# Second graph layer of a fused GNN + mixture-of-experts kernel: every engine's steps written out in an order of its own

## The reference

```
h = (_layernorm(x) * rsqrt(deg_out)); agg = segment_sum(h[src], dst)
h = (agg * rsqrt(deg_in)) @ W + b
x = x + gelu(_layernorm(h) * gamma + beta)                 # third sub-layer
xn = _layernorm(x); idx1 = argmax(xn @ w_gating)           # fourth: the expert of each row
pos1 = rank of the row among the rows with the same expert # its slot
out = x + gate1 * (gelu(_layernorm(xn) * gamma @ w1[idx1]) @ w2[idx1])
```

## Time and profile before

| | us |
|---|---|
| median of the runs | 965.11 |
| the profiled execution, its own time | 967.83 |
| its span, first to last instruction | 966.1 |
| PE busy over the span | 854.0 (88%) |
| DVE busy | 576.1 (60%) |
| ACT busy | 368.2 (38%) |
| POOL busy | 216.9 (22%) |
| granted PE clock, mean over the span | 0.942 of 2.4 GHz |

### The profile page before, as it was taken

The page is one execution under the profiler, slowest core; times in us unless marked ns, Lnnn a source line. Parts: engine busy times, 40 slices in busy tenths (PEclk is TensorE's granted clock), DMA queues, the critical chain, the costliest instruction groups (busy, mean ns, idle before and its releaser), DMA issues.

```text
span 966.1 us, 15966 instructions
## 1 busy us (share of the span) xinstructions
PE 854.0 (88%) x5064; PEld 572.6 (59%) x5064; DVE 576.1 (60%) x1871; ACT 368.2 (38%) x674; POOL 216.9 (22%) x425
## 2 busy tenths in 40 slices
PE   5989988989999999999997299999749999862996
PEld 2455554447777777777776277777414457452664
DVE  7488888338888787777773245555435325793121
ACT  1233434446665666666653133443200022231332
POOL 5000000000022012210222322222156213554443
PEclk9989999999999999999998599999959999965999
DMA  8239999972221024111008545653133440524550
GB/s 248 95 96 248 271 241 259 262 193 79 57 72 48 28 85 161 49 29 48 23 23 277 187 128 150 174 156 98 66 87 86 128 142 8 187 65 111 150 179 27
DMA packets 86979, 121.27 MB, mean 126 GB/s; under 512 B 40269, under 2 KB 49645, under 8 KB 86637
## 3 DMA queue, kind: packets, MB, share of 16 engines
q1 hardware_dynamic: 73293, 102.08, 38.0%
q0 software_dynamic: 13600, 18.11, 6.6%
HBM read 65.78 MB, written 57.08 MB: 127 GB/s over the span
## 4 chain that ended last, share of the span: by engine, by line
PE 72%; DVE 10%; issue 5%; DMA 4%; ACT 3%; POOL 3%; SPq 2%; DVEq 0%; POOLq 0%; ACTq 0%
PE ps L680 17%; PE ps L573 10%; PE ps L602 10%; PE ps L744 9%; PE ps L584 7%; PE ps L474 6%; PE ps L687 4%; PE ps L431 2%; PE ps L769 2%; DVE R_B L1419 2%; SPq L281 1%; DVE R_A L1517 1%; ACT R_B L893 1%; ACT R_A L888 1%; PE ps L639 1%
## 5 line engine op out<-in xcount | busy, mean ns | idle before, releaser
L680 PE MATMUL ps<-R_B,R_A 128*128 x612 | 186.0, 446 | 3.0 <-ACT R_A L1099 1.1
L680 PEld LDWEIGHTS ps<-R_B,R_A 128*128 128x128 f32 x612 | 111.9, 194 | 34.7 <-issue 24.6
L959 ACT ACTIVATE R_A<-R_A,neg_max 125x1250 f32<-125x1250 f32 x80 | 106.6, 1332 | 58.0 <-DVE neg_max L1517 58.0
L1517 DVE CUSTOM_DVE_ANT_0 R_A<-ps,R_B,neg_max 125x417 f32<-125x417 f32 (+1 forms) x160 | 97.6, 648 | 27.9 <-PE ps L573 27.9
L573 PE MATMUL ps<-R_B 64*125 64x417 f32 (+1 forms) x480 | 106.5, 544 | 2.8 <-ACT XN L912 1.5
L602 PEld LDWEIGHTS ps<-R_W,XN 125*64 125x64 f32 x1600 | 85.3, 136 | 23.9 <-issue 23.8
L584 PE MATMUL ps<-ident,R_A 125*125 125x125 f32 x800 | 98.7, 278 | 0.0
L584 PEld LDWEIGHTS ps<-ident,R_A 125*125 125x125 f32 x800 | 94.9, 188 | 1.5 <-DVE R_W L1524 0.7
L602 PE MATMUL ps<-R_W,XN 125*64 125x125 f32 x1600 | 94.7, 272 | 0.8 <-DVE counted L1571 0.8
L966 ACT ACTIVATE R_W<-ps 125x500 f32<-125x500 f32 x120 | 66.1, 585 | 51.1 <-PE ps L584 51.1
L474 PE MATMUL ps<-XT,R_W 128*128 128x512 f32 (+1 forms) x192 | 78.2, 557 | 0.8 <-ACT XT L899 0.8
(11 more groups left out here) (238 smaller groups left out, 1133.7 us busy)
## 6 DMA issues: line engine op xcount, KB each, us to landing
slots_d<-R_B SPq DMA_DIRECT2D x9, 2322.0 KB, 13.8
R_B<-in_L_ffn_w_dram SPq DMA_DIRECT2D x28, 512.0 KB, 6.5
R_A<-slots_d SPq DMA_DIRECT2D x27, 256.0 KB, 2.8
slots_d<-R_A SPq DMA_DIRECT2D x27, 256.0 KB, 2.4
counts_d<-R_A SPq DMA_DIRECT2D x10, 546.9 KB
logs_d<-R_B SPq DMA_DIRECT2D x10, 546.9 KB
R_B<-logs_d SPq DMA_DIRECT2D x10, 546.9 KB
R_B<-counts_d SPq DMA_DIRECT2D x10, 546.9 KB
```

Of the source, the lines that this page charges most:

```text
L680: ins = pe.matmul(bank(b, TM, width), lhs[:, c * TM:c * TM + TM], flat[:, bass.ds(e * (n * width) + c * width, width)], start=c == 0, stop ...
L959: act.activation(SC[u % 2][h], SC[u % 2][h], ACT.Exp, bias=neg_max[:, 2 * (u % 2) + h:2 * (u % 2) + h + 1], scale=-1.0, accum_out=den[:, 2 ...
L1517: dve.tensor_tensor_reduce(SC[u % 2][h][:, a:z], bank(2 * h + g % 2, P, z - a), LNB[i % 2][:, a:z], -1.0, least if t else 3.0e38, ALU.add, ...
```

## The change

The loops of the stage are replaced, on PE, ACT, POOL and DVE, by one call per line in a fixed order. `scale_shift` becomes `centre_rows` and `shift_rows`; `add_bias` and `add_layer` lose their statistics to `hidden_stats` and `layer_stats`; `pick_one` becomes `take_logits1`, `best_of`, `index_of`, `number_of` and `mask_of`; `next_norms` becomes `unit_root` and `unit_rms`. Where `link` made DVE wait at once for its own instruction, `mark` notes the semaphore's value and the step that needs the result waits for it. `add_bias(j)` now waits on DVE's own semaphore for `add_layer(j-3)`. No computation is added or left out. The scaled rows, the slot steps and the conditions of `project`, `aggregate_rest` and `scaled_rows` are as before; the wait for all of `AGT` moves into `turn_unit(0)`.

```diff
@@ -771,16 +768,14 @@
                 ins.then_inc(S("hg_made"), 1)
             pe.wait_ge(S("wg_in"), 16)
-            project(0)
-            for j in range(1, 5):
-                project(j)
-                aggregate_rest(j - 1)
             pe.wait_ge(S("gate_in"), 32)
             def turn_unit(i):
+                if i == 0:
+                    pe.wait_ge(S("agt_moved"), 3 * C)
                 pe.wait_ge(S("xn_made"), 2 * T + i + 1)
                 above_zero(pe, S("xt_moved"), 2 * T + i - 1 if i > 1 else 2 * T)
                 for c in range(C):
...
-            for k in range(5):
-                project(5 + k)
-                if k == 0:
-                    pe.wait_ge(S("agt_moved"), 3 * C)
-                turn_unit(k)
-                if k > 0:
-                    route_unit(k - 1)
-                if k > 1:
-                    rank_unit(k - 2)
-            for k in range(5, 8):
-                turn_unit(k)
-                route_unit(k - 1)
-                rank_unit(k - 2)
+            project(0)
+            project(1)
+            project(2)
+            project(3)
+            project(4)
+            project(5)
+            project(6)
+            aggregate_rest(0)
+            aggregate_rest(1)
+            aggregate_rest(2)
+            aggregate_rest(3)
+            project(7)
+            turn_unit(0)
+            turn_unit(1)
+            route_unit(0)
+            project(8)
+            turn_unit(2)
+            route_unit(1)
+            rank_unit(0)
+            route_unit(2)
+            turn_unit(3)
+            project(9)
+            turn_unit(4)
+            rank_unit(1)
+            route_unit(3)
+            turn_unit(5)
+            turn_unit(6)
+            route_unit(4)
+            route_unit(5)
+            route_unit(6)
+            rank_unit(2)
+            turn_unit(7)
             route_unit(7)
+            turn_unit(8)
+            rank_unit(3)
+            rank_unit(4)
+            route_unit(8)
+            turn_unit(9)
+            rank_unit(5)
+            route_unit(9)
             rank_unit(6)
-            turn_unit(8)
-            route_unit(8)
             rank_unit(7)
-            turn_unit(9)
-            route_unit(9)
             rank_unit(8)
             rank_unit(9)
...
-            for j in range(C):
-                hidden_gelu(j)
-                move_aggregate(2, j)
-                if j:
-                    unit_rows(j - 1)
-            for j in range(C, 7):
-                hidden_gelu(j)
-                move_unit(j - C)
-                unit_rows(j - 1)
+            def move_rest(c):
+                move_aggregate(2, c)
+            hidden_gelu(0)
+            hidden_gelu(1)
+            hidden_gelu(2)
+            unit_rows(0)
+            unit_rows(1)
+            hidden_gelu(3)
+            move_rest(0)
+            move_rest(1)
+            unit_rows(2)
+            hidden_gelu(4)
+            hidden_gelu(5)
+            unit_rows(3)
+            move_rest(2)
+            unit_rows(4)
+            hidden_gelu(6)
+            move_rest(3)
+            move_unit(0)
+            move_unit(1)
+            move_unit(2)
             hidden_gelu(7)
             move_unit(3)
+            unit_rows(5)
             unit_rows(6)
             move_unit(4)
             hidden_gelu(8)
+            unit_rows(7)
             move_unit(5)
             move_unit(6)
-            unit_rows(7)
+            hidden_gelu(9)
             move_unit(7)
-            hidden_gelu(9)
-            for j in range(8, T):
-                unit_rows(j)
-                move_unit(j)
+            unit_rows(8)
+            move_unit(8)
...
+            def unit_rms(j):
+                r, q = rstd[0:P, j:j + 1], inv_out[:, j:j + 1]
...
+            def number_rows():
...
+            hidden_root(0)
+            unit_root(0)
+            hidden_root(1)
+            hidden_root(2)
+            unit_root(1)
+            hidden_root(3)
+            hidden_root(4)
+            unit_rms(0)
+            hidden_root(5)
+            unit_root(2)
+            hidden_root(6)
+            unit_rms(1)
+            unit_root(3)
+            unit_rms(2)
+            unit_rms(3)
+            unit_root(4)
+            unit_rms(4)
+            unit_root(5)
+            unit_rms(5)
+            hidden_root(7)
+            unit_root(6)
+            unit_rms(6)
+            hidden_root(8)
+            number_rows()
+            scatter_unit(0)
+            unit_root(7)
+            unit_rms(7)
+            hidden_root(9)
+            scatter_unit(1)
+            unit_root(8)
+            unit_rms(8)
+            scatter_unit(2)
+            unit_root(9)
+            scatter_unit(3)
+            scatter_unit(4)
+            unit_rms(9)
+            scatter_unit(5)
+            scatter_unit(6)
+            scatter_unit(7)
+            scatter_unit(8)
+            scatter_unit(9)
...
+            def mark(ins):
+                c[0] += 1
+                ins.then_inc(S("dve_chain"), 1)
+                return c[0]
+            made_by = {}
             def add_bias(j):
                 dve.wait_ge(S("hg_made"), j + 1)
+                if j >= 3:
+                    dve.wait_ge(S("dve_chain"), made_by["layer", j - 3])
                 dve.scalar_tensor_tensor(HG[j % 3], bank(4 + j % 4, P), inv_in[:, j:j + 1], BIAS[0:P, :],
                                          ALU.mult, ALU.add).then_inc(S("hg_biased"), 1)
+            def hidden_stats(j):
                 dve.wait_ge(S("hg_biased"), j + 1)
                 link(dve.bn_stats(stats[0:P, j, :], HG[j % 3]))
                 dve.bn_aggr(mv[0:P, j, :], stats[0:P, j, :]).then_inc(S("hg_stat"), 1)
-            def scale_shift(j):
+            def centre_rows(j):
                 dve.wait_ge(S("hg_stat"), j + 1)
-                link(dve.scalar_tensor_tensor(HG[j % 3], HG[j % 3], mv[0:P, j, 0:1], GAMMA[0:P, :],
-                                              ALU.subtract, ALU.mult))
+                made_by["centre", j] = mark(
+                    dve.scalar_tensor_tensor(HG[j % 3], HG[j % 3], mv[0:P, j, 0:1], GAMMA[0:P, :],
+                                             ALU.subtract, ALU.mult))
+            def shift_rows(j):
+                dve.wait_ge(S("dve_chain"), made_by["centre", j])
                 dve.wait_ge(S("hg_rstd"), j + 1)
                 dve.scalar_tensor_tensor(HG[j % 3], HG[j % 3], rstd[0:P, j:j + 1], BETA[0:P, :],
                                          ALU.mult, ALU.add).then_inc(S("hg_shift"), 1)
             def add_layer(j):
                 dve.wait_ge(S("hg_gelu"), j + 1)
-                link(dve.tensor_tensor(X[:, j, :], X[:, j, :], HG[j % 3], ALU.add))
+                made_by["layer", j] = mark(dve.tensor_tensor(X[:, j, :], X[:, j, :], HG[j % 3], ALU.add))
+            def layer_stats(j):
+                dve.wait_ge(S("dve_chain"), made_by["layer", j])
                 row_stats(X, j)
...
-            def pick_one(i):
+            def take_logits1(i):
                 dve.wait_ge(S("log1_made"), i + 1)
                 dve.tensor_copy(logits[:, i, 0:E1], bank(2, P, E1)).then_inc(S("log1_taken"), 1)
+            def best_of(i):
                 dve.wait_ge(S("log1_taken"), i + 1)
-                link(dve.max(top[:, i, :], logits[:, i, :]))
-                link(dve.max_index(top_i[:, i, :], top[:, i, :], logits[:, i, :]))
-                link(dve.tensor_copy(pick[:, i, 0:1], top_i[:, i, 0:1]))
+                made_by["best", i] = mark(dve.max(top[:, i, :], logits[:, i, :]))
+            def index_of(i):
+                dve.wait_ge(S("dve_chain"), made_by["best", i])
+                made_by["index", i] = mark(dve.max_index(top_i[:, i, :], top[:, i, :], logits[:, i, :]))
...
-            for j in range(T):
-                add_bias(j)
-                if j in PICKED_EARLY:
-                    take_slots(RANKED_EARLY[j])
-                    pick_one(PICKED_EARLY[j])
-                scale_shift(j)
-                if j:
-                    add_layer(j - 1)
-                if j > 2:
-                    scaled_rows(j - 3)
-                if j in RANKED_LATE:
-                    take_slots(RANKED_LATE[j])
-                if j in PICKED_LATE:
-                    pick_one(PICKED_LATE[j])
-            add_layer(T - 1)
-            scaled_rows(T - 3)
+            add_bias(0)
+            hidden_stats(0)
+            centre_rows(0)
+            shift_rows(0)
+            add_bias(1)
+            add_layer(0)
+            layer_stats(0)
+            hidden_stats(1)
+            add_bias(2)
+            centre_rows(1)
+            hidden_stats(2)
+            shift_rows(1)
+            add_bias(3)
+            centre_rows(2)
+            hidden_stats(3)
+            add_layer(1)
+            layer_stats(1)
+            add_bias(4)
+            shift_rows(2)
+            hidden_stats(4)
+            add_layer(2)
+            add_bias(5)
+            centre_rows(3)
+            centre_rows(4)
+            scaled_rows(0)
```

(170 more changed lines are left out.)

## The result

The changed kernel takes 979.88 us (median of 4 runs, 978.69 to 983.4) against 963.94 us of the kernel before in the same comparison (4 runs, 962.49 to 965.93): 1.0154 times as long, 95% interval 1.0126 to 1.0183. That is 15.9 us more by the medians. The profiled execution took 983.40 us, span 981.7, against 967.83 and 966.1.

What follows compares the result with a forecast made beforehand. It took a wait chain through PE to 818.94, then dense DVE, to the tenth scatter at 881.41. Half clock gave +7.6, full +1.0; taking +6 gave 973.8 profiled, 971.1 median, range 962.0 to 977.0.

Steps and rivals of the forecast that it cites:

- +1.0 (full clock): Sum's low case: PE's late turns, routes and ranks at full clock, tenth scatter at 882.4 against 881.41.
- +7.6 (half): Sum's high case: PE's tail at half clock from 866, tenth scatter at 889.0 against 881.41.
- The stop at `scaled_rows(0)`: On DVE: due at 809.2, it waits for PE's fourth rest-aggregate until 826.0, standing still 16.8 us.
- Bias 9: DVE's add_bias after project 9: expected at 861.2 to 863, taken as 862.5, with 20.5 us of DVE work remaining.
- The half clock: PE's tail: granted clock 0.50 from about 866, some 3 to 5 us after project 9; routes 1.81 instead of 0.94.
- The waits for POOL's factors: On DVE: scaled_rows(1) waits 2.4 us for its factor behind POOL's hidden_root(6), scaled_rows(3) 0.8 for the same reason.
- PE up to 829 us: PE from 786.32: projects 0 to 6 end at 810.4, four rest-aggregates at 825.7, project 7 at 829.1; projects' waits don't bite.
- the three signs of being wrong: Wrong if DVE's stop is below 14 us, bias 9 comes before 859, or the tenth scatter starts before 880.
- rival B: Same DVE stop, but PE at full clock from project 8 on: +1 (966.1), no change that can be told; chance 0.25.
- Rival C (DVE catches up): DVE bounds the stage, fewer than half of the 10 us of waits appear: -6, 959; chance 0.15.
- The named waits: DVE after 826: 10 us of waits for POOL's factors, add_layer(6)'s gelu, logits 0 and project 8.
- Picks as single steps: On DVE: a pick falls from 1.02 toward about 0.5 us where its parts stand apart.

Runs made afterwards that it cites:

- e1: The changed kernel with PE's wait for the gating weights moved from ahead of project 0 to route 0, their first user: 976.03 us, ratio 1.0066 to before.
- e2: The kernel before with only PE's wait for the gating weights moved up ahead of project 0: 978.29 us, ratio 1.0083 to before.
- e4: The changed kernel, early wait kept, with SP issuing the gating weights ahead of the W1 and gamma loads: 974.55 us, ratio 1.0076 to before.
- b1: The change's split steps in another order, DVE doing everything that needs no rest-aggregate before scaled_rows(0), gate wait in route 0: 955.70 us, ratio 0.9858 to before.
- p1: m1 with only DVE's pick and slot steps spread between wide operations: 966.93 us, ratio 0.9998 to before.
- m1: The change's split steps called in the order of the kernel before, gate wait in route 0: 967.32 us, ratio 0.9983 to before.
- c3: e1 with 20 surplus matmuls, results unused, on PE between project 7 and the first turn: 973.98 us, ratio 1.0053 to before.
- c2: b1 with 4 surplus matmuls ahead of route 4 and single ones ahead of route 8 and ranks 5 to 9: 958.16 us, ratio 0.9904 to before.

## Why the prediction was wrong in size

- **The stage from project 0 on came out near the forecast, in part by luck.** +6 was said, from a range of +1.0 (full clock) to +7.6 (half). The changed kernel's part is +6.87, and e1, which is the change without the gate wait, +6.4 by its ratio (0.66% of 969.51). The stop at `scaled_rows(0)` was 16.80 against 16.8. Bias 9 came 871.31 - 792.27 - 2.74 = 76.3 us after project 0, forecast 76.2. The half clock came about where it was said (866): routes take 1.82 from 876.5, which is 867.8 on the forecast's scale; that the fall would come 3 to 5 us after project 9 was said without a row for it (it came some 5 us after). Two terms on the way to bias 9 were off and cancelled. The waits for POOL's factors at `scaled_rows(2)` and `(3)` were 1.50 and 1.00, where one of 0.8 was said, so that project 9 started 1.4 us later than forecast (858.9 on its scale); but it ran at full clock, 3.44, where the sum had put about 5.
- **The step that failed is the first, "PE up to 829 us".** It set project 0's start at the 786.32 of the old trace and said that the projects' waits don't bite. I looked only at the waits inside `project` and not at the line between the old place of the calls and the new one. The diff shows it: calls taken out above `pe.wait_ge(S("gate_in"), 32)` and put in below. The rows that give its price were in the old trace: SP's issue of that load at 786.03 and its 6.7 us to landing, 792.7 in all, against a PE that is there at 786.32. 6 us of idle time and 2.7 of cold clock are missing from the sum, and e1, e2 and e4 show them as 8.5, 8.0 and 7.5 us. With them 6 + 8.7 = 14.7 us would have been forecast; the spans differ by 15.6. No rival had this wait, and none of the three signs of being wrong could show it: the stop was 16.80, bias 9 and the tenth scatter came late and not early. They all looked at what follows project 0.
- **The clock rule.** The Trainium skill's statement that activity releases the throttle ("TensorE: Matmul & The Clock Gate", Part 1) led to rival B, +1. For an idle stretch and for wide matmuls the traces agree (0.50 after 6.45 us of idle time, 1.00 again from some 5 us on). For turns, routes and ranks they don't: in b1 PE is busy 5.00 of 5 us from 850 to 855 with these alone, at 0.50. The forecast went by the row, and the row was right.
- **Rival C (DVE catches up)** needed fewer than 5 us of waits between 826 and the end. The named waits all came, and DVE waited 16.3 us in all. But that room was there is shown by b1.
- **"Picks as single steps" at half a microsecond each:** none of it reaches the end by itself (p1). The prediction leans on it in rival C, with 0.6 us or more per pick, which isn't the half of 1.02 that it estimates elsewhere.

Not settled: how much the half clock in the tail costs. No run held it at full level there. And which of b1's moves made its gain wasn't taken apart.

## What to carry to other kernels

When calls move in a program with one list per engine, look for every wait, load or flag that stands between the old line and the new, also those in no function: the price of each is its data's landing less the time at which the engine gets there, plus a cold PE if the gap is long (here 6 us and 2.7). In a written-out order, find the first operation that waits for a late result and ask what stands behind it that doesn't: here one `scaled_rows` nine places too early cost some 12 us, and moving it and one wait turned a loss of 1.5% into a gain of 0.6%. Splitting the steps gave nothing clear by itself (m1, p1); what it allows is another order. And let one of the signs of being wrong check the step that the sum takes for granted, here the time at which the stage begins.

## What the hardware showed that I had not expected

After 17.3 us of wide matmuls without a break came 2.3 us of narrow work with gaps of at most 0.7 us, PE busy 1.20 of 2 us; the granted clock then fell just after the next wide product had begun, and stayed at half level for some 3.5 us although PE was busy throughout (c3: project 8 took 5.37 instead of 3.44). A PE 99% busy with narrow matmuls and two wide ones stayed at half clock for 10 us (c2). The same 12 KB load took 6.6 us to land behind six of 512 KB and one of 256 KB, and 1.8 us when issued ahead of them (changed kernel, e4). And a gap of 6.45 us cost 2.7 us more in the product that followed it.
